# Routing inside the self-attention loop, with rows scattered per expert and read back as contiguous tiles

## The reference, cut to what matters

```
x = x + xattn(layernorm(x), ctx_768, ...)          # 16 heads of 64, 256 keys per batch entry
x = x + attn(layernorm(x), wq, wk, wv, wo)         # 16 heads of 64, causal, 64 rows per batch entry
h = layernorm(x)
probs = softmax(h @ router_kernel_DE)              # 8 experts
weights, indices = top_k(probs, 2)
full = sum over the two of one_hot(indices) * softmax(weights)
y_e = (silu(h @ gate_e) * (h @ up_e)) @ down_e     # 256 -> 512 -> 256, for each expert e
x = x + sum over e of full[:, e] * y_e
```

## Time and profile before

| what | value |
|---|---|
| median of 3 runs | 2329.88 us |
| the profiled execution | 2323.2 us, span 2321.5 us |
| PE busy | 2196.8 us, 95% |
| DVE, ACT, POOL busy | 1595.0, 1282.5, 845.0 us |
| self-attention, first and last matmul | 1242.0 and 1866.2 us |
| first turn of the router, first gate matmul of the experts | 1871.4 and 1956.9 us |
| last matmul of the experts, last issue of an add | 2308.8 and 2312.8 us |

### The profile page before, as it was taken

How to read it: one execution, slowest core, us unless ns; L and a number is a source line. 1 busy time by engine, 2 the same in 40 slices (tenths; PEclk the granted TensorE clock), 3 DMA queues, 4 the chain that set the end, 5 groups by cost and what they waited for, 6 DMA issues and landing times. The chain is left out here.

```text
span 2321.5 us, 55712 instructions
## 1 busy us (share of the span) xinstructions
PE 2196.8 (95%) x18992; PEld 1986.3 (86%) x18992; DVE 1595.0 (69%) x3594; ACT 1282.5 (55%) x3842; POOL 845.0 (36%) x1022
## 2 busy tenths in 40 slices
PE   6999999999999999999995999999999965999997
PEld 5899999999999999999995999999999853888886
DVE  6666676666667676766655889888888856445442
ACT  5555555555555555555544676666666621445443
POOL 3333333333333333333331222222222222767675
PEclk9999999999999999999997999999999986999998
DMA  4000000000000000000004000000000011443434
GB/s 116 19 20 27 9 27 27 18 27 9 27 18 27 9 27 27 18 27 9 14 6 155 1 20 18 9 18 9 18 9 18 10 48 43 105 81 82 103 51 114
DMA packets 62074, 82.52 MB, mean 36 GB/s; under 512 B 10000, under 2 KB 45584, under 8 KB 61872
## 3 DMA queue, kind: packets, MB, share of 16 engines
q1 hardware_dynamic: 49040, 63.47, 8.5%
q0 software_dynamic: 12960, 18.12, 4.7%
HBM read 59.80 MB, written 25.96 MB: 37 GB/s over the span
## 5 line engine op out<-in xcount | busy, mean ns | idle before, releaser
L412 POOL TENSOR_TENSOR p_sb<-p_sb,rinv 128x512 f32<-128x512 f32 x256 | 279.2, 1091 | 779.7 <-DVE rinv L757 779.7
L667 ACT ACTIVATE p_sb<-s_ps,nmax 128x256 f32<-128x256 f32 x512 | 238.4, 470 | 198.5 <-DVE nmax L733 194.6
L733 DVE TENSOR_REDUCE nmax<-s_ps 128x2 f32<-128x512 f32 x256 | 176.2, 688 | 185.8 <-PE s_ps L65 181.4
L914 POOL TENSOR_TENSOR sp_sb<-sp_sb,srinv 128x512 f32<-128x512 f32 x128 | 133.3, 1041 | 426.1 <-DVE srinv L1108 426.1
L1056 ACT ACTIVATE sp_sb<-sm_sb,snmax 128x128 f32<-128x128 f32 x512 | 199.3, 390 | 7.2 <-DVE snmax L1119 4.1
L754 DVE COPY pt_sb<-t_ps 128x512 f32<-128x512 f32 x256 | 176.8, 691 | 22.2 <-PE t_ps L555 8.4
L46 ACT ACTIVATE q_sb<-m_ps 64x256 fp32r<-64x256 f32 x256 | 96.9, 379 | 164.2 <-PE m_ps L65 160.4
L45 ACT CAST qk_hi<-qk_ps 128x512 fp32r<-128x512 f32 x218 | 129.8, 596 | 95.3 <-PE qk_ps L65 87.7
L555 PE MATMUL t_ps<-ident,p_sb 128*128 128x128 f32 x1024 | 153.7, 273 | 2.1 <-POOL p_sb L412 1.1
L555 PEld LDWEIGHTS t_ps<-ident,p_sb 128*128 128x128 f32 x1024 | 125.1, 141 | 31.7 <-issue 4.5
L638 ACT COPY v_sb<-v_ps 128x512 f32<-128x512 f32 x256 | 149.5, 584 | 1.5 <-PE v_ps L65 1.5
(11 more groups left out here) (303 smaller groups left out, 7571.5 us busy)
## 6 DMA issues: line engine op xcount, KB each, us to landing
ctx_raw<-in_ctx_t SPq DMA_DIRECT2D x32, 256.0 KB, 2.8
ctx_raw<-in_ctx_t SPq DMA_DIRECT2D x64, 128.0 KB, 2.9
x_ring<-in_x SPq DMA_DIRECT2D x16, 256.0 KB, 2.7
x_mid<-x_ring SPq DMA_DIRECT2D x16, 256.0 KB, 2.2
xn<-f_xn SPq DMA_DIRECT2D x16, 256.0 KB, 2.2
acc<-x_sb SPq DMA_DIRECT2D x16, 256.0 KB, 2.4
e_raw<-in_gate SPq DMA_DIRECT2D x8, 512.0 KB, 4.0
e_raw<-in_up SPq DMA_DIRECT2D x8, 512.0 KB, 5.0
```

The costliest lines, as they stand in the source:

```text
L412: nc.gpsimd.tensor_tensor(prob, prob, inv, ALU.mult).then_inc(norm_done, 1)
L667: ex = nc.scalar.activation(p_sb[:, k, b * J:(b + 1) * J], s_ps[1 - w][:, b * J:(b + 1) * J], ACT.Exp, bias=nmax[:, k, b:b + 1], scale=1.0 ...
L733: nc.vector.tensor_reduce(nmax[:, (p - 1) % 4, :], s_ps[1 - w][:].rearrange("p (b j) -> p b j", b=2), AX_X, ALU.max, negate=True).then_inc ...
L914: nc.gpsimd.tensor_tensor(prob, prob, inv, ALU.mult).then_inc(norm_done, 1)
```

## The change

The router's stage is gone. Its work is done by group inside self-attention's loop, three groups behind: at p = 6 ACT normalises the rows of group g - 2 (`normed`) into `rows`, at p = 7 PE turns them (`turn_final`), and in the next group ACT copies, PE multiplies by the router's weights in plain float32 (`logits`, p = 1), DVE, ACT and POOL choose the experts (p = 1 to 4), PE counts the rows before each row (`prefix`, p = 5) and POOL makes the slots (`slots_of`, p = 6) and the weights (p = 0). POOL's part is 29 small instructions per group, linked one to the next. Two more steps later POOL scatters the rows: four indirect DMAs of 128 rows per group (two tiles, two experts each) write row, weights and row number (265 numbers) into a region of DRAM of 4096 slots per expert. The last three groups are done during and behind the drain, on DVE (`top_two`, `gates_of`, `slots_late`, n = 4 tiles at once and then n = 2). All regions are filled with blank rows beforehand, by 14 DMAs in cross-attention's loop (34.7 MB in all).

In the expert stage SP reads each tile back as one contiguous piece (`load_tile`). POOL only adds. The weights of expert 0 are loaded during self-attention and split by ACT and DVE when the expert stage begins. In DVE's tile `move(i + 2)` stands behind the split of the weights.

```diff
--- before.py
+++ after.py
...
+        xs_dram = nc.dram_tensor("xs", (EXPERTS * CAP + MAX_TILES * P, ROW), F32, kind="Internal").ap()
+        xs_tiles = xs_dram.rearrange("(t p) r -> t p r", p=P)
+        blank_dram = nc.dram_tensor("blank_rows", (P, ROW), F32, kind="Internal").ap()
...
+                sp.dma_start(blank_dram, pt_sb[:, 4, 0:ROW]).then_inc(s_blank, DMA)
...
+                    sp.dma_start(xs_tiles[bass.ds(FILL * g - 2 * FILL, FILL)],
+                                 blank_dram.unsqueeze(0).to_broadcast([FILL, P, ROW])).then_inc(s_fill, DMA)
...
+                def slots_of(g):
+                    pool.wait_ge(s_place, g + 1)
+                    for k in range(2):
+                        link(g, 17 + k, G.tensor_tensor(hs8[:, k], hot[:, k], place[:], ALU.mult))
+                    link(g, 19, G.tensor_tensor(hs4[:], hs8[:, :, :, 0:4], hs8[:, :, :, 4:8], ALU.add))
+                    link(g, 20, G.tensor_tensor(hs2[:], hs4[:, :, :, 0:2], hs4[:, :, :, 2:4], ALU.add))
+                    wait(pool, s_scat, 4 * DMA * g)
+                    link(g, 21, G.tensor_tensor(hs1[:], hs2[:, :, :, 0:1], hs2[:, :, :, 1:2], ALU.add))
+                    G.tensor_tensor(r_gate2[:], zero[:], zero[:], ALU.add)
+                    link(g, 22, G.tensor_copy(slot[:], hs1[:]))
...
+                    if p == 0 and not old:
+                        weights_of(past, x)
+                    if p == 1 and not old:
+                        if isinstance(G_, int) and G_ == 4:
+                            pool.wait_ge(s_fill, DMA * (FILLS + 2))
+                        dma_gate(past)
+                        for k in range(2):
+                            scatter(slot[:, k, 0], rows[:, x, 0, :])
+                    if p == 3 and not old:
+                        for k in range(2):
+                            scatter(slot[:, k, 1], rows[:, x, 1, :])
+                    if new:
+                        return
+                    if p == 2:
+                        first_choice(g)
+                    if p == 4:
+                        second_choice(g)
+                    if p == 5:
+                        gap_of(g)
+                    if p == 6:
+                        slots_of(g)
...
                         if p == 7 and not first:
+                            wait(pool, s_xf, 2 * g - 2)
                             ln_rstd(pool, ln_f, g - 1)
+                            if not drain:
+                                pool.wait_ge(ln_f["s_rstd"], g)
+                                G.tensor_tensor(shift_f[:], ln_f["mv"][:, :, 0], ln_f["rstd"][:], ALU.mult).then_inc(s_shift, 1)
+                                pool.wait_ge(s_shift, 2 * g - 1)
+                                G.tensor_tensor(shift_f[:], zero[:].to_broadcast([P, 2]), shift_f[:], ALU.subtract).then_inc(s_shift, 1)
+                        if drain and p in (5, 6):
+                            if p == 5:
+                                pool.wait_ge(s_late, 1)
+                                dma_gate(LATE)
+                            for k in range(2):
+                                scatter(late[4]["slot"][:, k, p - 5:p - 4], rows[:, LATE % 2, p - 5, :])
...
+                for u in range(2):
+                    for k in range(2):
+                        scatter(late[4]["slot"][:, k, 2 + u:3 + u], rows[:, 2, u, :])
+                pool.wait_ge(s_late, 2)
+                dma_gate(LATE + 1)
+                for u in range(2):
+                    for k in range(2):
+                        scatter(late[2]["slot"][:, k, u:u + 1], rows[:, 3, u, :])
...
+                        if p == 1 and cur and not (isinstance(g, int) and g < 3):
+                            pe.wait_ge(v_done, 4 * g + 1)
+                            logits(g - 3, v_ps, 0, 0)
...
+                        if p == 5 and cur and not (isinstance(g, int) and g < 3):
+
+                            pe.wait_ge(s_rp, OPS * (g - 3) + BOTH)
+                            pe.wait_ge(v_done, 4 * g + 3)
+                            prefix(v_ps, 2 * EXPERTS, both, 2)
+                        if p == 7 and cur and not (isinstance(g, int) and g < 2):
+                            pe.wait_ge(v_done, 4 * g + 4)
+                            turn_final(g - 2, x)
...
+                def turn_final(g, s):
+
+                    pe.wait_ge(s_xf, 2 * g + 2)
+                    for d in range(DC):
+                        for u in range(2):
+                            mm = pe.transpose(v_ps[:, (2 * d + u) * P:(2 * d + u + 1) * P],
+                                              rows[:, s, u, d * P:(d + 1) * P], ident[:])
+                    mm.then_inc(fx_mm, 1)
...
+                    for t in range(n):
+                        for s in range(t + 1):
+                            pe.matmul(bank[:, c0 + t * EXPERTS:c0 + (t + 1) * EXPERTS], (before if s == t else ones)[:],
+                                      of[:, s, :], start=(s == 0), stop=(s == t))
+                    for s in range(n):
+                        mm = pe.matmul(tot, ones[:], of[:, s, :], start=(s == 0), stop=(s == n - 1))
+                    mm.then_inc(pre_mm, 1)
...
+                def normed(g, s):
+
+                    act.wait_ge(s_shift, 2 * g + 2)
+                    for u in range(2):
+                        nc.scalar.activation(rows[:, s, u, 0:D], x_sb[:, bass.ds(2 * g + u, 1), :].rearrange("p u d -> p (u d)"),
+                                             ACT.Identity, bias=shift_f[:, u:u + 1],
+                                             scale=ln_f["rstd"][:, u:u + 1]).then_inc(s_xf, 1)
+
+                def final_copy(g):
+                    act.wait_ge(fx_mm, g + 1)
+                    wait(act, lg_mm, g)
+                    nc.scalar.copy(final_t[:].rearrange("p d t -> p (d t)"), v_ps[:]).then_inc(fx_copied, 1)
...
+                        if p in (2, 3) and cur and not (isinstance(g, int) and g < 3):
+                            best(g - 3, p - 2)
+                        if p == 5 and cur and not (isinstance(g, int) and g < 3):
+                            placed(g - 3, v_ps, 2 * EXPERTS, place, 2, s_place, g - 2)
+                        if drain and p == 3:
+                            top_two(0)
+                        if drain and p == 4:
+                            gates_of(0)
+                        if drain and p == 5:
+                            slots_late(0)
...
+                def load_tile(i, row, landed):
+                    sp.dma_start(xs_in[:, bass.ds(i % 2 * ROW, ROW)],
+                                 xs_tiles[bass.ds(row, 1)].rearrange("t p r -> p (t r)")).then_inc(landed, DMA)
+
+                sp.wait_ge(s_scat, 4 * GROUPS * DMA)
+                sp.wait_ge(s_fill, DMA * (GROUPS - 1))
+                load_tile(0, 0, s_xs)
+                load_tile(1, 1, s_xs_second)
+                sp.wait_ge(s_wlo, PIECES)
+                load_expert(sp, 1)
+                start = 0
+                for e in range(EXPERTS):
+                    bound = dict(min_val=MIN_TILES * (e + 1), max_val=MAX_TILES - MIN_TILES * (EXPERTS - 1 - e))
+                    end = sp.value_load(first_tile[0:1, e + 1:e + 2], **bound)
+                    shift = sp.value_load(region[0:1, e:e + 1], min_val=0, max_val=TILES * e) if e else 0
+                    for i in range(0 if e else 2, MIN_TILES):
+                        sp.wait_ge(s_moved, start + i)
+                        load_tile(start + i, start + i + shift, s_xs)
+                    if e + 2 < EXPERTS:
+                        sp.wait_ge(s_wlo, PIECES * (e + 2))
+                        load_expert(sp, e + 2)
+                    with sp.Fori(start + MIN_TILES, end) as i:
+                        sp.wait_ge(s_moved, i)
+                        load_tile(i, i + shift, s_xs)
+                    start = end
...
                     wait(pool, s_added, DMA * i)
-                    nc.gpsimd.tensor_tensor(token_out[:], token_of[:, bass.ds(i, 1)], none[:], ALU.add).then_inc(s_out_now, 1)
+                    pool.wait_ge(s_weight, i + 1)
+                    wait(pool, s_copy_gate, i)
+                    nc.gpsimd.tensor_tensor(copy_gate[:], zero[:], zero[:], ALU.add).then_inc(s_copy_gate, 1)
+                    nc.gpsimd.tensor_copy(token_out[:], weight[:, bass.ds(i * TAGS + EXPERTS, 1)]).then_inc(s_out_now, 1)
...
                     xt_lo_copy(i + 1)
-                    move(i + 2)
                     if piece is not None:
                         dve.wait_ge(s_whi, PIECES * (e + 1) + piece + 1)
                         cut = slice(piece * CUT, (piece + 1) * CUT)
                         split_lo_dve(nc, w_lo[:, (e + 1) % 2, cut], raw[:, cut], w_hi[:, (e + 1) % 2, cut]).then_inc(s_wlo, 1)
-
+                    move(i + 2)
...
```

More of the change, by code:

```diff
@@ L28 @@
 DMA = 16
+PARTS_OUT = 8
 def wait(eng, sem, value):
@@ new lines, in dma_gate, with scatter, route @@
+                def dma_gate(i):
+                    wait(pool, s_rgate, i)
```

(33 more changed lines are left out.)

722 lines of the change are left out of this document (377 added, 345 removed).

## The result

The changed kernel takes 2752.31 us (median of 4 runs, 2747.71 to 2753.16), the kernel before beside it 2329.15 us (4 runs): a ratio of 1.1816, 95% interval 1.1797 to 1.1836. The forecast was 2400 us, with a range of 2350 to 2445. The sign was right and the size was not.

| stretch | before | after | difference | forecast |
|---|---|---|---|---|
| start to first `sqk_ps` matmul (cross-attention) | 1250.3 | 1610.0 | +359.7 | 0 |
| to the start of the last `sy_ps` matmul (self-attention) | 615.6 | 644.9 | +29.3 | +30 |
| to the first `e_g_ps` matmul (the gap) | 91.0 | 37.2 | -53.8 | -57 |
| to the start of the last `e_y_ps` matmul (experts) | 351.5 | 439.9 | +88.4 | +99 |
| to the end | 13.1 | 19.4 | +6.3 | 0 |

What follows compares the result with a forecast made beforehand. PE, busy 95% of the span, was taken as the bound. 30 - 57 + 27 + 56 + 19 - 3 = +72 us gave 2395 on the profiled execution, 2402 on the median; forecast 2400 us, range 2350 to 2445.

Steps and rivals of the forecast that it cites:

- the fill of the regions runs beside cross-attention: Cross-attention: DMA engines under a tenth busy, some 75 us per 2.6 MB fill, so no added time.
- Self-attention, +30: Self-attention's loop: PE's new turns 7.4 us, logits 16.1, counts 5.2, plus 1.3 for waits; 30 us longer.
- The gap, -57: Between self-attention's last matmul and the experts' first gate matmul: the new chain ends 57.4 us earlier than the old.
- The split before the move, +27: Expert stage: DVE splits weights before moving the tile, so PE starts 1.78 us late in 15 tiles; 26.7 us.
- The load behind the weights, +56: Expert stage: SP's tile load queues behind the next expert's weights; PE loses 9.4 us six times, 56 us.
- Rival 1: Expert stage: the tile's load passes the weights, costing 35 us instead of 56; total +42, 2372 us; chance 0.20.
- The clock, +19: Expert stage: after each of the six long waits PE's clock is halved for 6.5 us, losing 3.2 us; 19 us.
- Gathers that leave, -3: Expert stage: without small late moves, 67 PE steps shorten by 0.05 us each; 3 us saved.
- Rival 2: Self-attention: POOL's scatters delay divisions, so PE waits 3 us more per group, 42 in all; 2442 us; chance 0.13.
- rivals 3 and 4: Expert stage: tile moves not held up, 2300 us, chance 0.07; drain and last three groups: over 60 us, adding 25.

Runs made afterwards that it cites:

- Experiments 1 to 4: Changed kernel with fills in 16 parts (2396.0 us), of 16 tiles (2396.14) or 18 (2395.51) instead of 19; kernel before with the 19-tile fills alone (2687.08).
- Experiment 11: Changed kernel with fill in 16 parts, six later experts' weights issued from ACT's queue, and DVE's move again before the split: 2312.77 us, ratio 0.9946.
- experiment 12: Changed kernel with fill in 16 parts; for five experts SP issues the tile's load ahead of the next weights, same wait: 2371.79 us, ratio 1.0187.
- experiment 10: Changed kernel with fill in 16 parts and six later experts' weights issued from ACT's queue, split still before move: 2343.13 us, ratio 1.0076.

## Why the prediction was wrong, point by point

- **The failed step: "the fill of the regions runs beside cross-attention ... I cost it at nothing."** It cost 359.7 us of the 429.9 in the spans. I had set its bytes against the room of all DMA engines and not asked how many of them carry it: one, for some 98 us, where the turn has 75. Experiments 1 to 4 settle this: with another outermost count the same bytes at the same place cost under 4 us. The Trainium skill, DMA: Bandwidth & Descriptors, section Why a DMA increments its semaphore by 16 and not by 1, has the rule: a DMA runs on the largest number of engines up to 16 that divides the slowest dimension (other than 1) of both its access patterns. By it 19 gives one engine. The runs agree in all four counts (19, 18, 16 and 13, by the packets and the landing times); I had read its neighbour section for the load behind the weights and not applied this one to the fill.
- **Self-attention, +30: measured +29.3,** in other parts than I said. PE's busy time grew by 23.8 us (606.8 to 630.7 over the stretch) where I had 28.7: the logits were 0.82 us and not 1.24, the counts 0.14 and not 0.4. With these, and the turns at the 0.53 of the forecast, the three parts add up to 19.9 us; 3.9 us of the busy time belong to none of them. The waits were 5.5 us and not 1.3 (`sy_ps` for the addition of `x_sb`, 5.7 us in 11 places). That the sum came out is luck: errors of 5 and 4 us cancel. No run took this loop apart, so the parts are read and not tested.
- **The gap, -57: measured -53.8,** and 36 to 37 us of gap in every variant. The steps up to the scatters come as forecast or earlier: the last rows are turned 9.2 us after the last `sy_ps` matmul (9.8 forecast), and the last scatter is issued at 23.7. The end is other than I said: SP's load of tile 0 waits for the end of the block (30.3 us after that matmul, where I had 28.3), and the split of expert 0's weights doesn't fit beside the load but holds the first move by 2.3 us. The first gate matmul comes at 37.2 and not at 33.6.
- **The split before the move, +27: confirmed.** The single wait is 1.69 us (1.78 forecast), so 15 of them are 25.4. Experiment 11 gives 31.4 for the order on DVE; it has the six tiles of the next term as well, which there wait for the split alone.
- **The load behind the weights, +56: confirmed.** The six waits are 9.28 to 9.85 us in the trace, 57.3 in all (9.4 each forecast), and the tile's load does come later behind the large ones (experiment 12). Rival 1 falls.
- **The clock, +19: about 12.** PE's busy time in the stretch is 353.4 us against 342.0 before. The half level lasted some 4 us into the work (2326.17 to 2330) and not 6.5. The waits of 1.7 us left the clock alone, as I had chosen: with them PE's busy time is 342.9 us (experiment 10), without them 341.8 (experiment 11).
- **Gathers that leave, -3: nothing.** With both costs taken out the stretch is 353.7 us against 351.5.
- **The tail, +6.3, was not in the sum.** The output's copies stand behind all of the tiles' loads in SP's program.
- Rival 2 (POOL breaks the loop) did not happen, nor rivals 3 and 4; a scatter's issue took 0.96 us. With the fill spread, the measured 2396.0 us stand beside the forecast of 2400. That closeness is partly luck too: there the expert stage cost 90 us and not 99, and the tail, 5 us longer, and cross-attention, self-attention and the gap, some 2 us over their terms each, make it good.

## What to carry to other kernels

Price a DMA by the engines that carry it: look at the outermost count of its pattern, and put a dimension with a multiple of 16 there. A transfer that "runs beside" something has to be checked in the windows for share and rate; a share of 0.06 is one engine, and whatever has a part on that engine waits, from another queue too when the pieces are long (51 KB here). Before a wait is put into a queue, name the next thing behind it that the critical engine needs; if there is one, issue it first or from another engine.

## What was unexpected of the hardware

- One DMA engine moved 27 GB/s between two places in DRAM in pieces of 34 KB, and 21 GB/s in pieces of 1 KB; all sixteen together up to 331 and 360 GB/s in two windows of the fill in 16 parts.
- The issue of a DMA can hold up the engine that issues it when much is outstanding: 11.6 us for a load behind one fill of 76 pieces, 73 us for a load behind a copy of 1824 pieces, up to 20.0 us on ACT for such a copy itself (1.29 us for the first, with none ahead of it).
- With pieces of 51 KB a store on another queue landed after 36 us, with pieces of 1 KB after 5.9: long pieces on one engine delay other queues too. Loads on another queue, issued 2 to 7 us behind such a copy, landed after 37.0 and up to 72.1 us.
